# Graph attention with two expert layers: the ten out-degree sums moved from even to odd units

## The reference

```python
x = x + _L0_gnn_ref(_layernorm(x), batch0, edge_index, W)    # q[src] . k[dst], softmax over the edges of src
...
deg_out = jnp.clip(jax.ops.segment_sum(ones, src, num_segments=n), 1.0)
deg_in = jnp.clip(jax.ops.segment_sum(ones, dst, num_segments=n), 1.0)
h = x * jax.lax.rsqrt(deg_out)[:, None]
agg = jax.ops.segment_sum(h[src], dst, num_segments=n)
```

## Time and profile before

| what | value |
|---|---|
| median of 3 runs | 852.57 us (851.87 to 854.69) |
| profiled execution | 853.61 us, its span 851.6 us |
| PE busy | 803.9 us (94%) |
| VectorE busy | 571.5 us (67%) |
| ScalarE busy | 395.4 us (46%) |
| chain that ended last | PE 75%, VectorE 12%, DMA 4%, POOL 3% |
| mean granted clock of TensorE | 0.983 of full speed |
| attention | about 166 to 487 us of the span |

### The profile page before, as it was taken

How to read it: one execution, slowest core, us unless ns; L and a number is a source line. 1 busy time by engine, 2 the same in 40 slices (tenths; PEclk the granted TensorE clock), 3 DMA queues, 4 the chain that set the end, 5 groups by cost and what they waited for, 6 DMA issues and landing times.

```text
span 851.6 us, 16427 instructions
## 1 busy us (share of the span) xinstructions
PE 803.9 (94%) x5245; PEld 550.0 (65%) x5245; DVE 571.5 (67%) x1869; ACT 395.4 (46%) x710; POOL 213.1 (25%) x382
## 2 busy tenths in 40 slices
PE   5998998999999999999999989999987999987996
PEld 2456555447777777877778766777755445666673
DVE  6479989546777988888778446555557835975121
ACT  1334444546667667676666533333331223533331
POOL 4200000000021122022022332222228822574443
PEclk9999999999999999999999989999999999997998
DMA  9909977688100443332483636555515470085550
GB/s 251 347 19 226 230 215 212 144 285 239 34 27 30 124 134 97 107 84 62 158 299 107 201 109 178 175 163 167 165 53 146 114 222 25 25 277 129 186 167 19
DMA packets 89029, 126.65 MB, mean 149 GB/s; under 512 B 41071, under 2 KB 50447, under 8 KB 88686
## 3 DMA queue, kind: packets, MB, share of 16 engines
q1 hardware_dynamic: 75342, 107.45, 42.5%
q0 software_dynamic: 13600, 18.11, 7.5%
HBM read 64.89 MB, written 63.33 MB: 151 GB/s over the span
## 4 chain that ended last, share of the span: by engine, by line
PE 75%; DVE 12%; DMA 4%; POOL 3%; issue 3%; ACT 1%; SPq 1%; DVEq 0%; POOLq 0%; ACTq 0%
PE ps L805 18%; PE ps L687 11%; PE ps L698 10%; PE ps L716 10%; PE ps L936 6%; PE ps L614 5%; DVE R_B L1922 4%; PE ps L812 4%; PE ps L619 4%; DVE R_B L1921 2%; PE ps L967 2%; DMA R_A<-slots_d 1%; PE ps L758 1%; DMA slots_d<-R_B,slot 1%; PE ps L555 1%
## 5 line engine op out<-in xcount | busy, mean ns | idle before, releaser
L805 PE MATMUL ps<-R_B,R_A 128*128 x612 | 184.1, 443 | 1.7 <-ACT R_A L1476 0.6
L805 PEld LDWEIGHTS ps<-R_B,R_A 128*128 128x128 f32 x612 | 110.9, 192 | 34.3 <-issue 24.5
L1281 ACT ACTIVATE R_A<-R_A,neg_max 125x1250 f32<-125x1250 f32 x80 | 106.4, 1330 | 19.1 <-DVE neg_max L1966 19.1
L1966 DVE CUSTOM_DVE_ANT_0 R_A<-ps,R_B,neg_max 125x417 f32<-125x417 f32 (+1 forms) x160 | 96.2, 648 | 21.2 <-PE ps L687 21.2
L698 PEld LDWEIGHTS ps<-ident,R_A 125*125 125x125 f32 x800 | 93.7, 188 | 14.8 <-issue 13.2
L698 PE MATMUL ps<-ident,R_A 125*125 125x125 f32 x800 | 102.0, 277 | 0.7 <-ACT XN L1224 0.7
L687 PE MATMUL ps<-R_B 64*125 64x417 f32 (+1 forms) x480 | 101.7, 536 | 0.2
L716 PE MATMUL ps<-R_W,XN 125*64 125x125 f32 x1600 | 94.7, 272 | 1.1
L716 PEld LDWEIGHTS ps<-R_W,XN 125*64 125x64 f32 x1600 | 85.5, 136 | 15.5 <-issue 14.2
L1288 ACT ACTIVATE R_W<-ps 125x500 f32<-125x500 f32 x120 | 66.1, 586 | 48.7 <-PE ps L698 48.7
L614 PE MATMUL ps<-XT,R_W 128*128 128x500 f32 (+1 forms) x192 | 72.4, 522 | 0.7 <-ACT XT L1207 0.7
(11 more groups left out here) (280 smaller groups left out, 1169.4 us busy)
## 6 DMA issues: line engine op xcount, KB each, us to landing
slots_d<-R_B SPq DMA_DIRECT2D x9, 2322.0 KB, 10.7
R_B<-in_L_ffn_w_dram SPq DMA_DIRECT2D x28, 512.0 KB, 8.2
R_A<-slots_d SPq DMA_DIRECT2D x27, 256.0 KB
slots_d<-R_A SPq DMA_DIRECT2D x27, 256.0 KB
counts_d<-R_A SPq DMA_DIRECT2D x10, 546.9 KB
logs_d<-R_B SPq DMA_DIRECT2D x10, 546.9 KB
R_B<-counts_d SPq DMA_DIRECT2D x10, 546.9 KB
R_B<-logs_d SPq DMA_DIRECT2D x9, 546.9 KB
```

The costliest lines, as they stand in the source:

```text
L805: ins = pe.matmul(bank(b, TM, width), lhs[:, c * TM:c * TM + TM], flat[:, bass.ds(e * (n * width) + c * width, width)], start=c == 0, stop ...
L1281: act.activation(SC[u % 2][h], SC[u % 2][h], ACT.Exp, bias=neg_max[:, 2 * (u % 2) + h:2 * (u % 2) + h + 1], scale=-1.0, accum_out=den[:, 2 ...
L1966: dve.tensor_tensor_reduce(SC[u % 2][h][:, a:z], bank(2 * h + g % 2, P, z - a), logs[:, a:z], -1.0, least if t else 3.0e38, ALU.add, ALU.m ...
```

## The change

The test that decides in which units a sum stands takes odd units and no longer even ones:

```diff
-                    if u >= OUT_DEGREE_AT and u % 2 == 0 and u < OUT_DEGREE_AT + 2 * T:
+                    if u >= OUT_DEGREE_AT and u % 2 and u < OUT_DEGREE_AT + 2 * T:
                         out_degree((u - OUT_DEGREE_AT) // 2)
```

## The result

The change makes the kernel slower by far more than forecast: 869.74 us (868.57 to 870.84) against 853.57 us (851.87 to 854.69) for the kernel before in the same comparison, a ratio of 1.018 [1.016, 1.021]. The forecast was 857.6, its range ended at 861.0. The profiled execution took 870.84 us with a span of 868.8, 17.2 us more than the 851.6 before. Busy time has hardly grown; what has is waiting and PE's slow clock.

What follows compares the result with a forecast made beforehand. PE was taken to set the pace. Stalls 2.4, logs of tile 9 2.4 and ScalarE 0.2 gave 5.0 us on the profiled 853.61, so 858.6; the median lies 1.04 lower, hence 857.6 us, range 854.8 to 861.0.

Steps and rivals of the forecast that it cites:

- The old places give nothing: Taking sums from their old units gains 0: four-unit windows last 30.55 us without and 30.56 us with two sums.
- L748's stalls, 5 x 0.48 = 2.4 us: Sums behind the normed row in units 13, 17, 21, 25, 29 delay a copy PE needs, 0.48 us each.
- the five waits for L1973: Sign: L748 waits 0.5 us for L1973 in units 14, 18, 22, 26 and 30, besides unit 38.
- Units 15 to 31: Sums in units 15, 19, 23, 27, 31 fit VectorE's 2.23 us idle behind the choice of two experts: cost 0.
- Logs of tile 9, 2.4 us: Last sum's release 8.8 us later makes logs late for unit 36's first negation; VectorE waits 4.0 us, PE stalls 2.4.
- The 0.8 us behind the last traffic: Time added from end of traffic until the logs are usable, taken from a plane store's end and SP's release.
- the bound of 3.5 us: Upper bound on PE's stall from the late logs of tile 9; the lower bound was 0.
- The clock rival: A stall of 2.4 us or more in unit 35 halves PE's clock: 857.6 + 3 = 860.6 us, chance 0.11.
- Work is dense on both sides: Argument against the clock falling: PE's work is dense before and after the long stall.
- The price of 3.4 us: Clock loss read from 494 to 502 in the earlier trace, granted clock 0.57: (1 - 0.57) x 8.
- ScalarE, 0.2 us: Conversions wait for later plane stores, 1.9 us late, just hidden; 0.1 us each in units 16 and 20.
- Logs 7 and 8, cost 0: Loads released later but about 6 us ahead of use, with 1.2 us slack: cost 0, up to 1 us.

Runs made afterwards that it cites:

- Experiment 8: Experiment 7 with the sums in units 12, 15, 16, 19, 20, 23, 24, 27, 28 and 31, never behind a normed row: 854.40 us, ratio 1.000.
- experiment 5: Experiment 1 with ScalarE's ten conversions one place later, in units 12, 14, ..., 30: 857.45 us, ratio 1.004.
- experiment 7: Experiment 5 with the loads of logs 7 and 8 issued one plane store earlier in SP's queue: 857.74 us, ratio 1.003.
- experiment 6: The changed kernel, with SP holding back the next three weight loads until the logs of tile 9 have landed: 869.93 us, ratio 1.017.
- experiment 10: The changed kernel, with logs 9 issued behind the eight W3E loads but ahead of the three of W1E: 861.36 us, ratio 1.013.
- experiment 1: The changed kernel, with the load of logs 9 issued ahead of the store of plane 9 and SP's wait for the sums: 860.16 us, ratio 1.008.
- experiment 4: The kernel before, sums in place, but the semaphore SP waits for raised one unit later by an empty instruction: 862.84 us, ratio 1.010.

## Why the prediction was wrong in size and right in kind

*The old places give nothing:* right. Experiment 8 puts half of the sums back and is as fast as before to 0.01 us in attention; the earlier trace rows told it.

*L748's stalls, 5 x 0.48 = 2.4 us:* right in mechanism and in the first stall (0.48 us in experiments 5 and 7), too small in sum: 3.3 us alone (experiment 7). The step that failed is the use of one place for five. The earlier trace rows already showed 0.73 us for such a stall; I noted it as the bound, and it was the better price for the later ones. Of the five waits for L1973 that were to show it, the change has four; unit 18 has none, and 0.71 us in experiment 5, where ScalarE does not wait.

*Units 15 to 31:* 0, right (experiment 8).

*Logs of tile 9, 2.4 us:* right in mechanism, wrong in size, and here most of the error lies: PE's pause is 6.4 us, and with the clock, for which the sum had nothing, units 35 and 36 lose 11.1. It failed in three steps. The release came 12.0 us later and not 8.8 (423.5 - 414.62 is 8.9, a slip of 0.1): PE had lost 5.8 and not 2.4 us by then, and a slower engine delays the sums which release the loads. The landing was taken as 22 us behind the release, as before, and took 25.8. That is slower transfer: the last packet of the logs ends 21.4 us behind the release before (at 441.22), 25.1 in the change and 23.3 in experiment 6; at most 1.2 us of it come from the loads that follow, and the cause of the rest is open. The 0.8 us behind the last traffic, which I took from a store's window, were no part of the error in the change, where 0.7 us pass; experiment 6 has 1.4. The Trainium skill (DMA: Bandwidth & Descriptors, Anatomy of one DMA) has about 2 us for the fixed cost, most of it the receipt, for transfers that GpSimd issues. These are SyncE's, and the traces have 0.4 us behind the last packet of the store and 0.7 and 1.4 behind that of the load. Third, the bound of 3.5 us took the other terms at their middle: a wait that is what remains of 26 us of queue behind a slack of 1 to 2 us takes every error of the terms before it in full.

*The clock rival, chance 0.11:* it held. It was set up for a pause of 2.4 us; with 6.4 us the clock did fall, for 4.6 us. It was no independent case but hung on the length of the stall: the traces have the fall with pauses of 4.0, 5.3 and 6.4 us, and none with 1.25 us (experiment 10). In the change it fell when PE had stood for 1.9 us, so the forecast pause of 2.4 us could have brought it down as well; what lies between was not tried. "Work is dense on both sides" spoke against nothing. The price of 3.4 us from the earlier trace rows took half speed for idle time too: PE was busy for 6.46 of the 8 us, which gives 2.8.

*ScalarE, 0.2 us:* a store does not end 6.1 us behind its release but 6.5 and 7.4 (285.56 to 292.05, 300.97 to 308.32), so conversions waited up to 3.1 us. Behind the second release SP also issues the logs of tile 5 (302.62), which I had not counted. The row for it:

```profile
308.32 1.25 ACT L1309 ACTIVATE R_A<-R_B 125x1250 bf16<-125x1250 f32 x1 [3.08 <-DMA planes_d<-R_A]
```

I also looked only at exponentials and blocks: `move_output` (L1304) stands behind a late conversion too, and PE's L758 waits for it. Experiments 1 against 5 price it at 0.4 us, too little to be told from the difference between traces.

*Logs 7 and 8, cost 0:* wrong, 0.7 us (experiments 5 against 7); their waits in the change are 1.2 and 1.6 us. They were inside the bound of 1 us that I had named.

The steps in attention: experiment 8 0.0, with the stalls 3.3 (7), with logs 7 and 8 4.0 (5), with conversions 4.4 (1), with logs 9 16.85 (some 1.3 of the last step is that one execution's). The sum of my terms was 5.0; without the logs of tile 9 the terms give 2.6 and the chip 4.4.

## What to carry to other kernels

An engine that is not the bound still carries releases. Ask first not what the moved work costs there, but which queue waits for its semaphore and how many bytes stand between that release and the next deadline: here five sums of 1.45 us cost 3.3 us, and the release one unit later cost 9.4 by itself (experiment 4) and 11.1 at one load in the change. A transfer that is needed soon should not stand behind a wait for something it does not need; one moved line (experiment 1) took back 12.4 of 16.85 us. And where a forecast has a pause of the matrix engine, its clock belongs into the same sum: a pause of 4 us cost 9 here, one of 6.4 us 11.

## What was not expected of the hardware

- PE's clock and pauses inside dense work. Pauses of 6.4, 5.3 and 4.0 us (the change, experiments 6 and 4) each brought the granted clock down from 1.00 to 0.50 while PE still stood: by windows of 0.1 us at 453.8, 454.0 and 450.4, when it had stood for 1.9, 3.1 and 3.6 us. It was back at full speed at 467.5, 464.2 and 460.7, when PE had been busy again for 9.2, 8.0 and 9.9 us. Beside the pause itself units 35 and 36 lost 4.6, 4.2 and 5.0 us more, about as much whatever the pause was. The pause of 1.25 us in experiment 10 shows no fall.
- The logs at the end of about 7 MB of traffic behind one release were usable after 22 us before (an estimate: 328 GB/s x 21.2 us = 6.9 MB, and 0.8), after 24.6 in experiment 6 (300 GB/s x 23.1 us = 6.9 MB, and 1.5), 24.9 in experiment 4 and 25.8 in the change. In the change the rate runs at 383 GB/s in the middle and at 242 over the last 8 us. There the logs are on their way, in rows of 1250 x 4 = 5000 bytes, and other loads with them:

```profile
441.00:449.50 8.50, 8.50 (x85) 6.26 (x83) 6.58 (x23) 5.31 (x10) 0.79 (x2) 1.00 1.07 383
449.50:457.50 8.00, 2.37 (x32) 1.53 (x28) 0.33 (x1) 2.23 (x5) 0.00 (x0) 0.77 1.03 242
```

  Whether the rows' length is the cause was not tried. Why the same bytes took 2 us more in experiment 6 than before stays open.
- The same program up to unit 34 is 4.4, 4.5, 4.6 and 5.8 us late in four kernels: where waits hang on DMA landings, one trace is uncertain by a microsecond or more.
